# Ten blocks of each tile turned by transposing DMAs of two blocks each, and the adjacency loaded 2048 columns at a time

## What is computed

```python
h = jnp.maximum(_layernorm(x, axis=-1), 0.0)            # x: 8192 x 128, fp32
scores = jnp.einsum('nd,md->nm', h, ks)                 # ks: 8192 x 128 -> 8192 x 8192
scores = jax.nn.leaky_relu(scores, negative_slope=0.2)
scores = jnp.where(adj > 0, scores, -9000000000000000.0)   # adj: 8192 x 8192 int32
attn = jax.nn.softmax(scores, axis=1)
x = x + jnp.einsum('nm,md->nd', attn, ks)
```

## Time and profile before

| | |
|---|---|
| median of the timed runs | 1596.42 us (1595.24 to 1597.04) |
| the profiled execution | 1591.91 us, of which the span from the first to the last instruction is 1590.0 us |
| PE busy | 1560.3 us, 98% of the span |
| DVE, ACT, POOL busy | 1418.5, 1342.3, 1329.5 us (89%, 84%, 84%) |
| granted TensorE clock | 0.998 |
| DMA | 437.67 MB, mean 275 GB/s |

### The profile page before, as it was taken

How to read it: one execution, slowest core, us unless ns; L and a number is a source line. 1 busy time by engine, 2 the same in 40 slices (tenths; PEclk the granted TensorE clock), 3 DMA queues, 4 the chain that set the end, 5 groups by cost and what they waited for, 6 DMA issues and landing times.

```text
span 1590.0 us, 37555 instructions
## 1 busy us (share of the span) xinstructions
PE 1560.3 (98%) x13202; PEld 1156.2 (73%) x13202; DVE 1418.5 (89%) x2527; ACT 1342.3 (84%) x2008; POOL 1329.5 (84%) x1348
## 2 busy tenths in 40 slices
PE   5899999999999999999999999999999999999998
PEld 3577777777777777777777777777777777777777
DVE  7998998999899899889889989998998998999896
ACT  6788888888888888888888888888888888888886
POOL 3688888888888888888888888888888888888885
PEclk9999999999999999999999999999999999999999
DMA  9999999999999999999999999999999999999995
GB/s 315 282 276 274 293 282 279 277 284 277 280 283 274 283 280 263 275 281 279 275 267 298 273 280 279 292 270 271 295 263 289 268 279 285 282 282 281 269 282 94
DMA packets 701626, 437.67 MB, mean 275 GB/s; under 512 B 629760, under 2 KB 629760, under 8 KB 701440
## 3 DMA queue, kind: packets, MB, share of 16 engines
q1 hardware_dynamic: 701440, 435.27, 112.7%
HBM read 276.82 MB, written 4.19 MB: 177 GB/s over the span
## 4 chain that ended last, share of the span: by engine, by line
PE 94%; DMA 1%; POOL 1%; DVE 1%; ACT 1%; issue 0%; POOLq 0%; DVEq 0%; ACTq 0%
PE ps_out L434 27%; PE ps_out L435 14%; PE ps_scores L408 13%; PE ps_scores L409 13%; PE ps_scores L407 13%; PE ps_T L418 12%; DMA keys_in<-keys_in 1%; PE ps_out L433 0%; PE ps_out L384 0%; ACT scores L505 0%; POOL keys_in L348 0%; POOL keys_in L346 0%; DVE scores L628 0%; PE ps_out L432 0%; ACT scores L496 0%
## 5 line engine op out<-in xcount | busy, mean ns | idle before, releaser
L348 POOL TENSOR_TENSOR keys_in<-scores,keys_in 128x512 f16<-128x512 f32 x572 | 720.6, 1260 | 46.1
L628 DVE CUSTOM_DVE_ANT_0 scores<-ps_scores,mask,minus_scale 128x1024 f32<-128x1024 f32 x512 | 653.9, 1277 | 16.1 <-PE ps_scores L409 1.2
L496 ACT ACTIVATE scores<-scores 128x1024 f32<-128x1024 f32 x512 | 538.0, 1051 | 77.9 <-DVE pair_min L628 77.9
L346 POOL CAST keys_in<-scores 128x512 f16<-128x512 f32 x572 | 460.0, 804 | 162.6 <-ACT scores L505 159.5
L505 ACT ACTIVATE scores<-scores,neg_max 128x1024 f32<-128x1024 f32 x512 | 583.4, 1140 | 0.1
L434 PE MATMUL ps_out<-keys,keys_in 128*128 128x256 f16 x2225 | 428.6, 273 | 3.1 <-DMA keys_in<-keys_in 3.1
L643 DVE TENSOR_TENSOR probsT_lo<-ps_T,probsT_hi 128x512 f16<-128x512 f32 x452 | 310.6, 687 | 123.6 <-ACT probsT_hi L513 114.9
L407 PE MATMUL ps_scores<-keysT_hi,hT_hi 128*128 128x512 f16 x1024 | 389.0, 380 | 13.9 <-DVE keysT_lo L599 9.7
L435 PE MATMUL ps_out<-keys,keys_in 128*128 128x128 f16 x2225 | 398.0, 219 | 0.0
L513 ACT ACTIVATE probsT_hi<-ps_T 128x512 f16<-128x512 f32 x447 | 264.5, 592 | 155.5 <-PE ps_T L418 152.1
L408 PE MATMUL ps_scores<-keysT_lo,hT_hi 128*128 128x512 f16 x1024 | 389.0, 380 | 0.0
(11 more groups left out here) (57 smaller groups left out, 825.7 us busy)
## 6 DMA issues: line engine op xcount, KB each, us to landing
adj_in<-in_adj_dram SPq DMA_DIRECT2D x512, 512.0 KB, 5.3
keys_in<-keys_in SPq DMA_TRANSPOSE x572, 5.6
x_in<-in_x_dram SPq DMA_DIRECT2D x16, 256.0 KB, 4.0
keys_in<-in_L_gnn_ks_dram SPq DMA_DIRECT2D x8, 512.0 KB, 7.1
out_dram<-out_tile SPq DMA_DIRECT2D x16, 256.0 KB, 4.1
keys<-keysT_hi SPq DMA_TRANSPOSE x8, 4.7
keys<-keysT_lo SPq DMA_TRANSPOSE x8, 4.6
```

The costliest lines, as they stand in the source:

```text
L346: nc.gpsimd.tensor_copy(half[:, 0:BLOCK], probs(t, b)).then_inc(half_hi_ready, 1)
L348: nc.gpsimd.tensor_tensor(half[:, BLOCK:2 * BLOCK], probs(t, b), half[:, 0:BLOCK], ALU.subtract) \
L496: nc.scalar.activation(s, s, ACT.Prelu, alpha=1.0 / SLOPE).then_inc(leaky_ready, 1)
L628: nc.vector.tensor_tensor_reduce(out=score_pair(q, p), in0=ps_scores[:, slots, :].rearrange("p s k -> p (s k)"), in1=mask[:, (p // 2) % 2, ...
```

## The change

`BY_DMA` gains block 4 (ten of sixteen), and in the last tile block 8 joins it. A transposing DMA now takes two blocks that are neighbours in the list: (1, 3), (4, 5), (7, 9), (11, 12), (13, 15), 128 x 2048 fp16 (512 KB) each. It is issued at the place of its second block, waits for that block's halves, and signals one semaphore for both. `D_SLOTS` goes from 8 to 10; `halves` keeps six slots, which are now released two at a time. PE uses a turned block one step later (`ADD_LAG` 11), and therefore `transpose_h`, `split_h` and `finish` each stand one step later. The adjacency is loaded 2048 columns (1 MB) at a time, at j = 1, 5, 9 and 13, with as much in flight ahead as before.

```diff
-    D_SLOTS = 8
+    D_SLOTS = 10
-    ADD_LAG = 10
+    ADD_LAG = 11
-    BY_DMA = tuple(b for b in range(BLOCKS) if b % 2 == 1 or b in (12,))
+    BY_DMA = tuple(b for b in range(BLOCKS) if b % 2 == 1 or b in (4, 12))
-    LAST_BY_DMA = (1, 3, 5, 7, 9)
-    LAST_BY_DVE = (0, 2, 4, 6, 8)
+    LAST_BY_DMA = (1, 3, 5, 7, 8, 9)
+    LAST_BY_DVE = (0, 2, 4, 6)
...
-            def load_adj(q, p):
-                n = q * PAIRS + p
-                if n >= 2 * ADJ_SLOTS:
-                    sp.wait_ge(mask_ready, n // 2 - ADJ_SLOTS + 1)
-                sp.dma_start(adj_in[:, n // 2 % ADJ_SLOTS, n % 2 * PAIR:(n % 2 + 1) * PAIR],
-                             adj_tiles[q // GROUP, q % GROUP, :, p * PAIR:(p + 1) * PAIR]).then_inc(adj_loaded[n % (2 * ADJ_SLOTS)], 16)
+            def load_adj(q, k):
+                n = q * LOADS + k
+                if n >= ADJ_SLOTS:
+                    sp.wait_ge(mask_ready, n - ADJ_SLOTS + 1)
+                sp.dma_start(adj_in[:, n % ADJ_SLOTS, :],
+                             adj_tiles[q // GROUP, q % GROUP, :, k * LOAD:(k + 1) * LOAD]).then_inc(adj_loaded[n % ADJ_SLOTS], 16)
...
-                sp.dma_start(turned[:, n % D_SLOTS, :, :], halves[:, n % R_SLOTS, :], transpose=True) \
-                    .then_inc(turned_in[n % D_SLOTS], 16)
+                to, of = (n - 1) % D_SLOTS, (n - 1) % R_SLOTS
+                sp.dma_start(turned[:, to:to + 2, :, :].rearrange("p s k c -> p (s k) c"),
+                             halves[:, of:of + 2, :].rearrange("p s k -> p (s k)"), transpose=True) \
+                    .then_inc(turned_in[to // 2], 16)
...
-                        q, p = divmod((i + 1) * PAIRS + j // 2 + 6, PAIRS)
-                        if q < TILES:
-                            load_adj(q, p)
+                        if j % 4 == 1:
+                            q, n = divmod((i + 1) * LOADS + j // 4 + 3, LOADS)
+                            if q < TILES:
+                                load_adj(q, n)
...
-                        if turning:
-                            turn(*turning)
+                        if turning and nth_dma(*turning) % 2 == 1:
+                            turn_two(*turning)
...
-                    pool.wait_ge(turned_in[m % D_SLOTS], 16 * (m // D_SLOTS + 1))
+                    pool.wait_ge(turned_in[m % D_SLOTS // 2], 16 * (m // D_SLOTS + 1))
...
-                    if j == 12 and ahead:
+                    if j == 13 and ahead:
                         transpose_h(i + 2, odd)
...
-                    if ahead and j == 13:
+                    if ahead and j == 14:
                         split_h(i + 2, odd)
...
-                    if prev and j == 10:
+                    if prev and j == 11:
                         finish(i - 1, 1 - odd)
```

More of the change, by code:

```diff
@@ L117, in gat_kernel @@
         ps_out = psum("ps_out", [P, 2, BLOCK], fp32)
-        adj_loaded = [sem(f"adj_loaded{s}") for s in range(2 * ADJ_SLOTS)]
+        adj_loaded = [sem(f"adj_loaded{s}") for s in range(ADJ_SLOTS)]
         keys_loaded = [sem(f"keys_loaded{p}") for p in range(PAIRS)]
@@ L158, in gat_kernel @@
         half_lo_ready = sem("half_lo_ready")
-        turned_in = [sem(f"turned_in{s}") for s in range(D_SLOTS)]
+        turned_in = [sem(f"turned_in{s}") for s in range(D_SLOTS // 2)]
         out_done = sem("out_done")
@@ L252, in store, with turn_two @@
                 sp.dma_start(out_groups[g], out_tile[:, g % 2, :, :]).then_inc(stored, 16)
-            def load_adj(q, p):
-                n = q * PAIRS + p
-                if n >= 2 * ADJ_SLOTS:
-                    sp.wait_ge(mask_ready, n // 2 - ADJ_SLOTS + 1)
-                sp.dma_start(adj_in[:, n // 2 % ADJ_SLOTS, n % 2 * PAIR:(n % 2 + 1) * PAIR],
-                             adj_tiles[q // GROUP, q % GROUP, :, p * PAIR:(p + 1) * PAIR]).then_inc(adj_loaded[n % (2 * ADJ_SLOTS)], 16)
-            def turn(t, b):
+            def load_adj(q, k):
[4 more added lines that the diff above has]
+                             adj_tiles[q // GROUP, q % GROUP, :, k * LOAD:(k + 1) * LOAD]).then_inc(adj_loaded[n % ADJ_SLOTS], 16)
+            def turn_two(t, b):
                 n = nth_dma(t, b)
@@ L282, in _ @@
                              key_runs[:, 2 * p:2 * p + 2, :, :]).then_inc(keys_loaded[p], 16)
-            for p in range(6):
-                load_adj(0, p)
+            for n in range(3):
+                load_adj(0, n)
             load_x(1)
@@ L351, in make_first_mask @@
             def make_first_mask(k):
-                pool.wait_ge(adj_loaded[2 * k], 16)
-                pool.wait_ge(adj_loaded[2 * k + 1], 16)
+                pool.wait_ge(adj_loaded[k], 16)
                 pool.wait_ge(mask_ready, k)
@@ L449, in output_turned @@
                 n = nth_dma(t, b)
-                pe.wait_ge(turned_in[n % D_SLOTS], 16 * (n // D_SLOTS + 1))
+                pe.wait_ge(turned_in[n % D_SLOTS // 2], 16 * (n // D_SLOTS + 1))
                 for k in range(PER_BLOCK):
@@ L605, in make_mask @@
                 n = q * LOADS + k
-                dve.wait_ge(adj_loaded[2 * (n % ADJ_SLOTS)], (n // ADJ_SLOTS + 1) * 16)
-                dve.wait_ge(adj_loaded[2 * (n % ADJ_SLOTS) + 1], (n // ADJ_SLOTS + 1) * 16)
+                dve.wait_ge(adj_loaded[n % ADJ_SLOTS], (n // ADJ_SLOTS + 1) * 16)
                 if q > 0 or k >= 2:
```

## The result

The changed kernel took 1781.78 us (median of four runs, 1773.79 to 1784.08) beside 1596.06 for the kernel before: 1.1154 times as long, 95% interval 1.1119 to 1.119. It is 186 us slower where 18 us of gain were forecast, and far above the range. The profiled execution has a span of 1778.7 us, 189 more than before. Over 63 tiles that is 3.0 us a tile, on top of 24.09.

A forecast was written before the change was run, and what follows sets the result against it. PE was taken to bound at 24.09 us a tile; afterwards POOL's 23.69 plus a tenth, 23.78. From 1591.9, 19.5 off and 1.5 on gave 1573.9, plus 4.5 carried over: 1578 us, own range 1567 to 1588, overall 1566 to 1612.

The forecast's parts named there:

- PE's 0.44 us a tile: On PE: block 4's four transposes go, saving 0.44 us a tile, 28.2 us in all; PE alone 23.65 a tile.
- POOL's 23.69: On POOL: 21.85 us of work a tile plus 1.84 for splitting a tenth block, now above PE's 23.65.
- The DMA side has some 0.6 us a tile to spare: SP's DMA queue: read as nearly full, with two gaps of 0.22 and 0.42 us in one tile as its room.
- the DMA share of 1.16: Profile row of the kernel before, beside 278 GB/s: taken as support that the DMA side has little to spare.
- The price of the tenth block: DMA side: 256 KB more a tile costs 1.23 us (the shortest issue), bounds 0.72 and 1.75.
- It must save 1.0 us a tile … since half the changeovers go: DMA queue: fewer, larger DMAs must save 1.0 us a tile to stay below 23.78; called the least certain term.
- Loads of 1 MB … nothing: Adjacency loads: each is issued some eleven steps, 16 us, before its mask is made, so widening costs nothing.
- The landing: Turned pairs reaching PE, tightest at block 7: 8.1 us of room against 6.8 expected; mostly hidden, longest 9.5 does not fit.
- the DMA side becomes the bound: Rival, DMA queue from SP's issue to landing: a tile needs 24.2 to 24.7 us; 1622 us (1604 to 1638), chance 0.23.
- the sign that the prediction named for it: SP's queue: turnings take over 4 us each to issue and PE waits for every pair.
- The estimate of 21.7 us: DMA side: ten turnings 10.0 us plus adjacency 11.7 by the skill page's rates, so DMA would not bound.

The follow-up runs named there:

- e5: Changed kernel with single turnings and 1024-column loads, every second load cut to 64 columns (half the adjacency bytes): 1567.9 us, ratio 0.9795.
- e6: Kernel before with block 12 given back to PE, so eight blocks turned by DMA, loads of 1024 columns: 1620.4 us, ratio 1.0124.
- e2: Changed kernel without pairing and wide loads: ten blocks turned one at a time, loads of 1024 columns: 1677.8 us, ratio 1.0545.
- e16: Kernel before with loads of 2048 columns and block 12 given back to PE, eight blocks turned singly: 1624.0 us, ratio 1.0193.
- e11: Changed kernel with ten single turnings and loads of 512 columns, half of them behind the turnings: 1703.3 us, ratio 1.0677.
- e4: Changed kernel with single turnings in place of pairs, loads of 2048 columns kept: 1793.0 us, ratio 1.1274.
- e1: Kernel before with only the adjacency loads widened to 2048 columns, nine blocks turned one at a time: 1697.3 us, ratio 1.0666.
- e7: Kernel before with 2048-column loads issued from ACT's queue in place of SP's, nine single turnings: 1856.3 us (one execution), ratio 1.160.
- e9: Kernel before with its 1024-column loads issued two in a row at the places of the wide loads: 1637.8 us, ratio 1.0261.
- e15: Changed kernel with ten single turnings and 1024-column loads, each load issued behind the turnings of its step: 1704.9 us, ratio 1.0687.
- e14: Kernel before with each 512 KB load filling 64 partitions with 8 KB rows in place of 128 with 4 KB: 2067.1 us, ratio 1.297.
- e17: Kernel before with each 512 KB load filling 64 partitions with two separate 4 KB rows, columns permuted: 2081.4 us, ratio 1.3007.
- e8: Changed kernel with the adjacency loads issued from ACT's queue in place of SP's: 1898.9 us, ratio 1.1862.

## Why the prediction was wrong

*PE's 0.44 us a tile, POOL's 23.69, and what hangs on them: right.* e5 and e6 show both. The saving was there and lay off the path that sets the end.

*"The DMA side has some 0.6 us a tile to spare": wrong, and the step on which the rest fell.* It was read from two gaps in SP's queue in one tile. What the runs give directly is the price of the tenth block less the room for it: 1.38 us a tile (e2), where the prediction had 1.23 - 0.6 = 0.63. By the account above 0.14 of it was room. The gaps are no measure of room: with eight blocks there are 7.7 us of them a tile (e6), with nine 0.7, so one turning of some 1.5 us took up 7. Nor were there only two gaps in that tile: a third of 0.20 us stands before the store at 1027.83. And the DMA share of 1.16, which "speaks for it", does not separate a full DMA side from one with room: from 1000 to 1100 us it is 1.11 in the changed kernel and 1.10 in e16.

*The price of the tenth block: undersized.* 1.23 us was taken, from the shortest issue. That is how long SP needs to issue a turning, not how long the DMA side needs to move it: e11 has a median issue of 1.24 us and a DMA side that holds up PE. The cost by the account is 1.52 us, a little nearer to the median issue of 1.75, but e4 and e11 show that the median is no price either.

*"It must save 1.0 us a tile … since half the changeovers go": wrong.* It was the term called least certain, and it had no row. With narrow loads pairing cost 0.7 us a tile; with wide ones it saved 0.25 to 0.3, a quarter of what was asked. What the doubled DMA itself saves (13 us a run) is less than what its later place costs (58).

*"Loads of 1 MB … nothing": wrong by 1.7 us a tile, the largest error.* It asked only when the load must be there, and there were 16 us of room. It never asked how much of the shared DMA time it takes, and no wait for `adj_in` stands in the view of waits: it is the turnings behind a load that pay. Nor did any rival hold this mechanism, which is why the slower one ended at 1638.

*The landing: half right.* Median 7.3 us where 6.8 were expected and 8.1 available. But the stall shown above took 8.77, of which 5.40 was the issue: the landing can't be forecast apart from the queue.

*The rival "the DMA side becomes the bound"* had the place right. For the tenth block alone its 24.2 to 24.7 us a tile, 0.1 to 0.6 over PE's 24.09, fell short of the 25.5 measured in e2, 1.38 over. With chance 0.23 it was the only one that forecast a slower kernel, and the sign that the prediction named for it came: pairs issued in over 4 us each, and PE and POOL waiting for them. The estimate of 21.7 us by the Trainium skill (DMA: Bandwidth & Descriptors, "Latency and other measured facts") is for a tile that took 25.5 on the DMA side in e2: the page's two rates, each for one kind of DMA, did not add up to the time of the mixture here. The same page, under "Bandwidth", asks for DMAs of 1 MiB or more, on measurements of loads from HBM alone. Beside turnings the measurement decides otherwise: 1697 us with 1 MB loads, 1591 with 512 KB.

In sum, from the runs: 87 us for the tenth block, 106 for the wide loads, 9 more for both at once, and 16 to 19 less by the pairing, which with wide loads helps a little: 183 to 186, where 186 were measured. What stays open is what inside the DMA side makes a later, longer or differently ordered DMA dearer; the runs give the prices, not the mechanism.

No run beat the kernel before while reading the whole adjacency. The account says why: both sides are nearly full at nine blocks, 24.09 and some 23.95 us. A tenth block has 0.4 us a tile to give and asks for 1.4.

## What to carry to other kernels

Before work is moved from a full engine to the DMAs, see whether the DMA side is full as well. A queue with hardly any gaps is a warning that what is moved there may be paid in full (0.7 us of gaps a tile before the change, 7.7 with one turning less); the median issue time is none (1.24 and 1.31 us in two kernels whose PE waited for turned blocks). The way to know is one run that cuts the bytes, or gives one transfer back, and leaves the rest (e5, e16). And when small DMAs with a deadline share a queue with bulk loads, keep the loads in small pieces between them: size, order and queue of the loads alone were worth 21 to some 150 us here, with all bytes the same (e1, e7, e9, e11, e15), though below 512 KB nothing more was gained.

## What the runs showed of the hardware that was not expected

- Loads of 1 MB beside transposing DMAs moved 257 GB/s over the run, 512 KB loads 275, with the same bytes (e1, before). 256 KB loads, half of them behind the turnings, were no faster than 512 KB ones (e11, e2).
- The same 512 KB in 64 partitions in place of 128 landed in 7.3 us in place of 5.3 and took the run from 1594 to 2067 us (e14), whatever the row length (e17).
- The issue of a transposing DMA on SP took 1.23 us for one block and 1.68 for two at the shortest, and 1.75 and 5.18 in the median: its median does not tell how full the queue is, since it was 1.31 us in e4 (1793 us) and 1.24 in e11 (1703 us), where PE waited for turned blocks, and 1.75 before, where it did not.
- Two queues for the same DMAs were worse than one, by some 113 and 149 us (e8, e7).
- After PE had been busy 2.43 of 5 us the clock was granted at 0.52 for 3 us (after): that wait cost PE more than its own length.
